# The older graph's last layer moved beside the last graph's layers, and ten repeated mask matmuls between layers, in a fused four-layer graph network kernel

## The reference

```
x = layernorm(x + relu(attention(x, A)))          # 4 heads of 16, softmax over neighbours
x = layernorm(x + (A + I) x / rowsum(A + I))
x = layernorm(x + A (x W) + bias)
x = layernorm(x + (t / t where t = A x > 0.5, else 0))
```

## Time and profile before

| | us |
|---|---|
| median of 3 runs | 1536.1 (1535.46 to 1537.45) |
| the profiled execution | 1531.98 |
| its span, first to last instruction | 1529.9 |
| PE busy | 1343.7 (88%) |
| DVE busy | 1266.8 (83%) |
| ACT busy | 1223.3 (80%) |
| POOL busy | 1035.5 (68%) |
| mean granted PE clock | 0.946 of 2.4 GHz |

### The profile page before, as it was taken

One profiled execution on the slowest core, in us unless ns is written; L12 is line 12 of the kernel. 1 busy time (PEld: TensorE's weight loads), 2 busy tenths in 40 slices (PEclk: granted clock), 3 DMA queues, 4 the chain that ended last, 5 costly groups with the idle time before them and its releaser, 6 DMA issues. The chain is left out here.

```text
span 1529.9 us, 21041 instructions
## 1 busy us (share of the span) xinstructions
PE 1343.7 (88%) x7296; PEld 675.7 (44%) x7296; DVE 1266.8 (83%) x1490; ACT 1223.3 (80%) x1404; POOL 1035.5 (68%) x562
## 2 busy tenths in 40 slices
PE   2788889998989988999989989999889999899856
PEld 1443334544445544444545544454445444355323
DVE  2677998897888889898888889988898988988864
ACT  1587888887988878898888878988788888888731
POOL 3067777787677776778677776778767776867412
PEclk7898999999999999999999999999999999999978
DMA  6624552434424442425325344245424343200000
GB/s 94 111 34 63 61 79 52 68 41 48 90 43 63 57 65 56 54 61 52 72 62 75 34 49 89 45 60 59 66 62 58 53 47 69 54 15 16 26 10 11
DMA packets 140879, 84.95 MB, mean 56 GB/s; under 512 B 100372, under 2 KB 130522, under 8 KB 140762
## 3 DMA queue, kind: packets, MB, share of 16 engines
q1 hardware_dynamic: 125542, 64.67, 20.1%
q0 software_dynamic: 14160, 18.51, 15.6%
q10 hardware_dynamic: 1072, 0.43, 0.1%
HBM read 103.33 MB, written 21.38 MB: 82 GB/s over the span
## 5 line engine op out<-in xcount | busy, mean ns | idle before, releaser
L533 POOL TENSOR_TENSOR LS<-LS,MB 125x1000 f32<-125x1000 f32 x372 | 860.7, 2332 | 368.2 <-DVE LS L934 272.2
L774 ACT ACTIVATE LS<-Z 126x1000 f32<-126x1000 f32 x576 | 575.1, 1000 | 150.6 <-PE Z L601 149.9
L782 ACT ACTIVATE LS<-LS 125x1000 f32<-125x1000 f32 x576 | 595.8, 1035 | 47.3 <-POOL LS L533 22.5
L920 DVE TENSOR_TENSOR RP<-LS,RP 125x1000 f32<-125x1000 f32 x480 | 575.6, 1199 | 45.0 <-ACT LS L774 19.4
L599 PE MATMUL Z<-AT,BI 126*126 126x500 fp8e4 x1152 | 367.2, 401 | 77.8 <-ACT LS L774 44.2
L601 PE MATMUL Z<-FS,FO 128*125 128x500 f16 x1152 | 348.8, 384 | 0.0
L628 PE MATMUL M<-LS,V 126*18 126x500 f32 x2304 | 315.9, 622 | 8.8 <-ACT LS L782 8.7
L934 DVE TENSOR_TENSOR LS<-LS,MB 125x1000 f32<-125x1000 f32 x204 | 319.9, 1573 | 0.1
L599 PEld LDWEIGHTS Z<-AT,BI 126*126 126x126 bf16 x1152 | 126.8, 138 | 376.6 <-issue 158.2
L683 PE MATMUL M<-AT,XP 125*128 125x500 fp8e4 x756 | 203.4, 378 | 3.6 <-ACTq L821 3.1
L601 PEld LDWEIGHTS Z<-FS,FO 128*125 128x125 f16 x1152 | 162.0, 141 | 92.4 <-issue 9.2
(11 more groups left out here) (133 smaller groups left out, 798.7 us busy)
## 6 DMA issues: line engine op xcount, KB each, us to landing
MB<-row_maxima SPq DMA_DIRECT2D x48, 500.0 KB, 4.1
adj_cast<-in_adj_dram POOLq DMA_DIRECT2D x96, 183.1 KB, 4.5
FO<-PARTS SPq DMA_DIRECT2D x120, 46.9 KB, 2.1
FS<-PARTS SPq DMA_DIRECT2D x120, 46.9 KB, 2.1
XF<-in_x_dram SPq DMA_DIRECT2D x8, 336.0 KB
XA<-in_x_dram SPq DMA_DIRECT2D x8, 336.0 KB
out_dram<-X SPq DMA_DIRECT2D x7, 375.0 KB
AT<-adj_cast SPq DMA_TRANSPOSE x144, 2.8
```

The source lines that it names most:

```text
L533: nc.gpsimd.tensor_tensor(rows, rows, MB[:P, u % 2, :, :], ALU.subtract).then_inc(sub_pool, 1)
L774: nc.scalar.activation(LS[:PD, q % RL, :, :], banks("Z", q)[:PD], ACT.Prelu, alpha=SLOPE).then_inc(bent, 1)
L782: nc.scalar.activation(rows, rows, ACT.Exp, scale=0.25).then_inc(exps, 1)
L920: nc.vector.tensor_tensor(run, rows, run, ALU.max).then_inc(maxed, 1)
```

## The change

Six edits. The last graph gets tiles of its own: its layer results go to XA and XF and LAST_MEAN and LAST_RSTD, instead of X, Y, MEAN and RSTD; the wait for the older store goes. Layer norm 3 of graph 6 (`(B - 2, 3)`) leaves the loop on all engines, and is placed between the last graph's layers: mean and centring (DVE) after the low parts of layer 0, the square (ACT, into LS slot 0) after layer 0's copies, sum and eps (`old_sums`) after layer 1's low parts, `power` (GpSimd) after layer 1's end powers, and scaling (`old_scale`, without the copy to M1) after layer 2's low parts. SP's store of graph 6 keeps its place in SP's order. The low parts of chunks 0 and 1 of layer 0 move to step 598, ahead of the last `keep`. PE waits for the last `keep` only before it writes the bank that this `keep` reads (`held`), and takes that bank last in the first chunk. And after layers 0 and 1 PE repeats a mask matmul of 500 columns ten times (`keep_clock`), whose result nobody reads.

```diff
+        LAST_MEAN = sb("LAST_MEAN", [P, NT], f32)
+        LAST_RSTD = sb("LAST_RSTD", [P, NT], f32)
+        OLD_SQ = LS[:P, 0, :, :].rearrange("p h c -> p (h c)")[:, 0:NT * F].rearrange("p (t f) -> p t f", f=F)
...
@@ layer_at
-                if off == 0 and 1 <= b < B:
+                if off == 0 and 1 <= b < B and (b, l) != (B - 1, 3):
                     return b - 1, l
...
@@ gpsimd
             for l in range(4):
                 for c in range(NS):
                     end_power(l, c)
+                if l == 1:
+                    power(B - 2, 3)
...
@@ tensor
+            def keep_clock(n):
+
+                for k in range(n):
+                    nc.tensor.matmul(RP[:PD, 0, 0:C], BI[:, :], AT[:P + 1, (NS * B - 1) % RS, 0, PAD:CP, 0], start=True, stop=True)
...
-            pe.wait_ge(kept_seq, 5 * NU)
+            held = place["G", NU - 1] % RZ
+            ring_free(place["G", NU - 1] + 1)
             parts = (YT, O4, REST)
             for l in range(3):
                 for q in range(NS):
                     pe.wait_ge(end_low, 3 * l + q + 1)
-                    for c in range(NS):
+                    for c in (1 - held, 2, held) if l == q == 0 else range(NS):
+                        if l == 0 and q == 0 and c == held:
+                            pe.wait_ge(kept_seq, 5 * NU)
...
                     last.then_inc(end_back, 1)
+                if l < 2:
+                    keep_clock(10)
...
@@ scalar, after layer l's copies
+                if l == 0:
+                    act.wait_ge(weighed, QN // 2)
+                    act.wait_ge(dve_seq, link_of(B - 2, 3, 1))
+                    nc.scalar.activation(OLD_SQ, Y[:, :, :], ACT.Square).then_inc(squared, 1)
...
@@ vector: in add, centred, summed, scaled, low_part of the last graph
-  X, Y, MEAN, RSTD
+  XA, XF, LAST_MEAN, LAST_RSTD   (also in end_highs, end_power and the last stores)
...
             def scaled(l, c):
                 rows = slice(ST * c, ST * (c + 1))
                 dve.wait_ge(end_rstd, 3 * l + c + 1)
-                if l == 0 and c == 0:
-                    dve.wait_ge(stored, 16 * (B - 1))
...
+            def old_sums():
+                dve.wait_ge(squared, 4 * (B - 1))
+                nc.vector.tensor_reduce(RSTD[:, :], OLD_SQ, AX.X, ALU.add).then_inc(dve_seq, 1)
+                dve.wait_ge(dve_seq, link_of(B - 2, 3, 2))
+                nc.vector.tensor_scalar(RSTD[:, :], RSTD[:, :], F * EPS, None, ALU.add).then_inc(var_ok, 1)
+
+            def old_scale():
+                dve.wait_ge(rstd_ok, 4 * (B - 1))
+                nc.vector.scalar_tensor_tensor(out=X[:, :, :], in0=Y[:, :, :], scalar=F ** 0.5,
+                                               in1=RSTD[:, :].unsqueeze(2).to_broadcast(bc3),
+                                               op0=ALU.mult, op1=ALU.mult).then_inc(x_ready, 1)
...
                 if q == LAST_ROWS + 2:
                     for c in range(NS - 1):
                         scaled(0, c)
+                if q == LAST_ROWS + 4:
+                    for c in range(NS - 1):
+                        low_part(0, c)
             normalise(0, NS - 1)
-            low_part(0, 0)
-            low_part(0, 1)
             scaled(0, NS - 1)
             low_part(0, NS - 1)
+            mean(B - 2, 3)
+            centre(B - 2, 3)
             for l in range(1, 4):
...
                 if l < 3:
                     low_part(l, NS - 1)
+                if l == 1:
+                    old_sums()
+                if l == 2:
+                    old_scale()
```

More of the change, by code:

```diff
@@ L555, in end_power @@
             def end_power(l, c):
-                part = RSTD[:, ST * c:ST * (c + 1)]
+                part = LAST_RSTD[:, ST * c:ST * (c + 1)]
                 pool.wait_ge(end_sum, 3 * l + c + 1)
@@ L1040, in add @@
                 bank = end_banks(c)[:, 1]
-                y, ps = Y[:, ST * c:ST * (c + 1), :], bank[:P, 0:ST * F].rearrange("p (t f) -> p t f", f=F)
+                y, ps = XF[:, ST * c:ST * (c + 1), :], bank[:P, 0:ST * F].rearrange("p (t f) -> p t f", f=F)
                 if l == 0:
@@ L1044, in add @@
                         t = ST * c + k
-                        ins = nc.vector.scalar_tensor_tensor(out=Y[:, t, :], in0=ps[:, k, :], scalar=RDEN[:, t:t + 1],
-                                                             in1=X[:, t, :], op0=ALU.mult, op1=ALU.add)
+                        ins = nc.vector.scalar_tensor_tensor(out=XF[:, t, :], in0=ps[:, k, :], scalar=RDEN[:, t:t + 1],
+                                                             in1=XA[:, t, :], op0=ALU.mult, op1=ALU.add)
                 elif l == 1:
-                    ins = nc.vector.tensor_tensor(y, ps, X[:, ST * c:ST * (c + 1), :], ALU.add)
+                    ins = nc.vector.tensor_tensor(y, ps, XA[:, ST * c:ST * (c + 1), :], ALU.add)
                 else:
-                    ins = nc.vector.scalar_tensor_tensor(out=y, in0=ps, scalar=0.5, in1=X[:, ST * c:ST * (c + 1), :],
+                    ins = nc.vector.scalar_tensor_tensor(out=y, in0=ps, scalar=0.5, in1=XA[:, ST * c:ST * (c + 1), :],
                                                          op0=ALU.is_gt, op1=ALU.add)
@@ L1056, in centred @@
                 rows = slice(ST * c, ST * (c + 1))
-                y = Y[:, rows, :]
+                y = XF[:, rows, :]
                 before = XA[:, rows, :] if l == 0 else y
@@ L1060, in centred @@
                     dve.wait_ge(kept_seq, 5 * (NU - NS + c + 1))
-                step(c, nc.vector.tensor_reduce(MEAN[:, rows], before, AX.X, ALU.add))
+                step(c, nc.vector.tensor_reduce(LAST_MEAN[:, rows], before, AX.X, ALU.add))
                 follow(c)
-                step(c, nc.vector.scalar_tensor_tensor(out=y, in0=MEAN[:, rows].unsqueeze(2).to_broadcast([P, ST, F]),
+                step(c, nc.vector.scalar_tensor_tensor(out=y, in0=LAST_MEAN[:, rows].unsqueeze(2).to_broadcast([P, ST, F]),
                                                        scalar=-1.0 / F, in1=before, op0=ALU.mult, op1=ALU.add))
@@ L1068, in summed @@
                 rows = slice(ST * c, ST * (c + 1))
-                y, squares = Y[:, rows, :], SQ[:, rows, :]
+                y, squares = XF[:, rows, :], SQ[:, rows, :]
                 step(c, nc.vector.tensor_tensor(squares, y, y, ALU.mult))
                 follow(c)
-                step(c, nc.vector.tensor_reduce(RSTD[:, rows], squares, AX.X, ALU.add))
+                step(c, nc.vector.tensor_reduce(LAST_RSTD[:, rows], squares, AX.X, ALU.add))
                 follow(c)
-                nc.vector.tensor_scalar(RSTD[:, rows], RSTD[:, rows], F * EPS, None, ALU.add).then_inc(end_sum, 1)
+                nc.vector.tensor_scalar(LAST_RSTD[:, rows], LAST_RSTD[:, rows], F * EPS, None, ALU.add).then_inc(end_sum, 1)
             def normalise(l, c):
@@ L1083, in scaled @@
                 dve.wait_ge(end_rstd, 3 * l + c + 1)
-                if l == 0 and c == 0:
-                    dve.wait_ge(stored, 16 * (B - 1))
-                nc.vector.scalar_tensor_tensor(out=X[:, rows, :], in0=Y[:, rows, :], scalar=F ** 0.5,
-                                               in1=RSTD[:, rows].unsqueeze(2).to_broadcast([P, ST, F]),
+                nc.vector.scalar_tensor_tensor(out=XA[:, rows, :], in0=XF[:, rows, :], scalar=F ** 0.5,
+                                               in1=LAST_RSTD[:, rows].unsqueeze(2).to_broadcast([P, ST, F]),
                                                op0=ALU.mult, op1=ALU.mult).then_inc(end_x, 1)
@@ L1092, in low_part @@
                 dve.wait_ge(end_high, 3 * l + c + 1)
-                nc.vector.tensor_tensor(XP[:, rows, F:2 * F], X[:, rows, :], XP[:, rows, 0:F],
+                nc.vector.tensor_tensor(XP[:, rows, F:2 * F], XA[:, rows, :], XP[:, rows, 0:F],
                                         ALU.subtract).then_inc(end_low, 1)
+            def old_sums():
[8 more added lines that the diff above has]
+                                               op0=ALU.mult, op1=ALU.mult).then_inc(x_ready, 1)
             for c in range(NS):
```

4 lines of the change are left out of this document (2 added, 2 removed).

## The result

The changed kernel took 1520.62 us in the median of four executions (1517.14 to 1521.59), the kernel before 1535.78 (four, 1534.29 to 1537.45): 15.2 us less, ratio 0.9897 with the interval 0.9881 to 0.9912. The profiled execution took 1521.29 us.

What follows compares the result with a forecast made beforehand. It took the DVE to bound the loop's last stretch, then PE in layer 0. 5.5 + 3.9 + 2.3 - 0.15 = 11.5 us off the median 1536.1 gave 1524.6 us, range 1521 to 1530.

Steps and rivals of the forecast that it cites:

- Step 1: End of the loop: taking the older layer out lets the last subtraction end earlier, a gain of 5.5 us.
- Steps 2 and 3: Last graph's layer 0: PE can start 5.92 us after the last subtraction, not 9.54; chunk 2 comes 0.8 us later.
- Step 4: PE in layer 0: DVE's first add comes at 1477.9 instead of 1487.32, 3.9 us of it from the earlier start.
- Step 5: The older layer's parts and store, placed between the last graph's layers, are all hidden and cost 0.
- Step 6: Between layers 0 and 1: ten repeated matmuls hold PE's clock through layer 1, gaining 2.3 us.
- rivals A to D: A, clock falls: 1526.9 us, 0.20; B, early start useless: 1528.4, 0.07; C, clock low: 1543.5, 0.03; D, parts unhidden: 1526.6-1528.6, 0.08.
- Step 7: Between layers 1 and 2: ten more repeated matmuls cost 0.15 us, as the clock held there without them.
- the main loop's: The 72-step main loop ahead of the tail: priced at nothing, with 3 us allowed for it in the range.

Runs made afterwards that it cites:

- keep_first: The changed kernel with only the ten repeated matmuls after layer 0, not those after layer 1; median 1523.42 us, ratio 0.9930 to the kernel before.
- keep_second: The changed kernel with only the ten repeated matmuls after layer 1, not those after layer 0; median 1521.95 us, ratio 0.9934 to the kernel before.
- no_keep: The changed kernel without any of the twenty repeated matmuls; median 1525.59 us, ratio 0.9940 to the kernel before.
- moved_only: The changed kernel without the early start of layer 0 and without the twenty repeated matmuls; ratio 0.9948 to the kernel before.
- before_keeps: The kernel before with only the ten repeated matmuls after each of layers 0 and 1 added; median 1532.55 us, ratio 0.9989.
- early_only: The kernel before with both low parts at step 598 and PE waiting for the last keep only before the bank it reads; ratio 0.9973.
- drain_keep: The changed kernel with five more repeated matmuls behind each of the last five weighings; ratio 0.9932 to the kernel before.
- low_later: As drain_keep, with the low part of chunk 1 behind the last keep instead of ahead of it; ratio 0.9918 to the kernel before.
- gap_fill: As drain_keep, with eight more repeated matmuls behind the last turned sums; ratio 0.9905 to the kernel before.

## Why the prediction was right or wrong

**Step 1** was right: T - G went from 11.11 to 5.55 us, 5.6 less where 5.5 was said, in the combined and in the single edit. **Steps 2 and 3** were right: PE at T+6.02 (T+5.92 said), the last low part at T+12.23 (T+12.45 said, so 0.6 us later than before and not 0.8), and the removed wait for the store gained nothing, as the power took its place. **Step 4** was right in its sum, first add 1477.9 by the clock of the old profile (1479.11 less the 1.26 us of the loop's shift). On the way there one thing was otherwise: it had the clock down from the drain on, and the clock was up at 1466 to 1467, fell again as PE began, and came back at T+9.1 and not T+9.8. How exactly the sum was met is in part luck: PE started 3.5 us earlier, with or without the other edits, and the rest of the 3.9 hangs on when the clock comes back. That was 3.9 to 4.3 us after PE's start in the three profiles of the old order and 2.8 to 3.4 in the four of the changed kernel, and the early start alone, with 4.4, gave 3.3. So the rise does move from execution to execution, as the prediction had it, and in the changed kernel it came earlier than in the old one, where the prediction allowed for later. **Step 5** was right: nothing of the older layer shows in the tail. **Step 6** was right: 7.96 us for 7.8, and 2.0 us by taking the ten away. So the rivals A to D fell.

**Step 7** took one row for a rule: "The clock held here without them." It holds in seven of eight profiles; the second ten cost 0.03 us at most, where 0.15 was said, and save 1.5 us in the eighth. If one in eight is the rate, that is some 0.2 us saved in the average of the executions (an estimate); the forecast had the cost alone. The runs' medians (1523.42 for keep_first, 1521.95 for keep_second, six executions each) leave room for more, and don't show it.

**The term that failed is the main loop's**: "I price the 72-step rhythm of the main loop at nothing, and allow for it in the range", with 3 us, "a little over the 2 us by which the three runs before differ". The mechanisms of the tail were right. Its sum was 11.5, and the profiles say 11.6. Outside the span the kernel before spends 2.07 us (mean of 12 executions), the changed one 1.76 (four): 0.3 us more, which no step had. It goes with the older layer's move (means of 1.74 in no_keep and 1.75 in moved_only, 2.07 in before_keeps and 2.09 in early_only); why isn't shown. That makes 12.0. The remaining 3.2 us of the first comparison (3.8 in the means) lie ahead of the tail: the spans less the tails put G at 1459.2 before in the mean (1535.83 - 2.07 - 71.08 - 3.45, 71.08 being the mean of the three tails) and at 1455.4 after (1519.99 - 1.76 - 59.34 - 3.45), where the instructions are the same. In the 17 profiles G moved from 1453.44 to 1462.19, nearly all of it in the first 400 us, and a load of the very same kernel stood 2.2 us above another. The allowance of 3 us downwards was therefore too small: three executions of one load don't tell where a kernel stands to better than some 2 us.

That chance is all of it isn't shown. Over all loads the means are 1534.1 us (101 executions) and 1519.7 (20), 14.4 apart, which is 2.4 more than tail and end explain, with a standard error of 0.7 if executions were independent, which the loads say they are not. Against a cause in the change: the seven other kernels with the moved layer (moved_only, no_keep, keep_first, keep_second, drain_keep, low_later, gap_fill) put G from 1.7 us before to 1.6 us after that of the kernel before in the same job, with a mean of 0.1 after, and the place of the two small tiles makes nothing faster. The steady loop is no faster either: from graph 0's last add to G it is 1053.45 us in the mean of the six profiles with the older layer in its old place and 1053.38 in the four of the changed kernel. A real part would have to lie in the first 400 us, where the profiles of either kind spread over several us. Whether a part of the 2.4 us is real stays open.

## What to carry to other kernels

Where the last units of a long loop drain, count what the busiest engine still does there for older work: here the 5.6 us that moved into later waits were gained in full, and the edits added up (6.3 + 3.2 + 1.8 us alone, 11.5 to 11.7 together). Replace a wait for everything by a wait at the one result that needs it. When a change touches the end only, compare profiles from the last common instruction, and widen a range on the total by what the common part does by itself, taken from several loads: here the first 400 us alone moved by 7.5.

## What the runs showed of the hardware

- The same 1.96 us without PE work dropped the clock in one profile and not in seven; 1.81 us, after 15.9 us of work without a stop, dropped it in both profiles that have it (drain_keep, low_later), and 1.15 us in none of nine. In the 3.27 us gap it fell in all eight. So near 2 us the length of the gap doesn't tell whether the clock falls; what does, these runs don't show, and a row that held once is no price.
- When the clock comes back moves from execution to execution too: 3.9, 3.9 and 4.3 us after PE's start of layer 0 in the old order, 2.8 to 3.4 in the changed one. Its products with A took 10.09 to 10.30 us and 9.56 to 9.84, with no edit within either group.
- Two loads of an identical program differed by 2.2 us in the mean, where the spread of the executions (standard deviations 2.4 and 1.9 us, 12 and 23 of them) gives a standard error of 0.8 us, and by 0.7 us in a second pair.
